# Layer 1 of a four-layer graph network: gathers by rows of 128 edges instead of by items, into a ring of 128 rows

## What is computed

```python
def _L1_gnn_ref(x, edge_index, W_msg, b_msg, W_upd, b_upd):
    messages = jax.nn.relu(x @ W_msg.T + b_msg)
    src, dst = (edge_index[0], edge_index[1])
    aggregated = jax.ops.segment_sum(messages[src], dst, num_segments=x.shape[0])
    updated = jax.nn.relu(aggregated @ W_upd.T + b_upd)
    return updated + x
# layer 2, on the result x: msg_in = concat(h[src], h[dst], edge_attr_64), two matmuls with a gate
...
h = jnp.maximum(_layernorm(x, axis=-1), 0.0)
x = x + _L1_gnn_ref(h, edge_index, L1_gnn_W_msg, L1_gnn_b_msg, L1_gnn_W_upd, L1_gnn_b_upd)
```

## Time and profile before

| | |
|---|---|
| median of 3 runs | 6709.26 us (6705.14 to 6719.22) |
| profiled execution, time | 6689.83 us |
| profiled execution, span | 6688.1 us |
| layer 1, edges: first gather issued to the node update's start | 1957.49 to 3217.80 us |
| layer 1, gathers: 832, first to last issue | 1957.5 to 3201.1 us |
| granted TensorE clock, mean of the execution | 0.755 |

### The profile page before, as it was taken

How to read it: one execution, slowest core, us unless ns; L and a number is a source line. 1 busy time by engine, 2 the same in 40 slices (tenths; PEclk the granted TensorE clock), 3 DMA queues, 4 the chain that set the end, 5 groups by cost and what they waited for, 6 DMA issues and landing times. The chain is left out here.

```text
span 6688.1 us, 110212 instructions
## 1 busy us (share of the span) xinstructions
PE 4492.3 (67%) x20750; PEld 3303.1 (49%) x20751; DVE 3446.8 (52%) x10783; ACT 1916.5 (29%) x5540; POOL 3778.8 (56%) x3395
## 2 busy tenths in 40 slices
PE   0588788888545555555767776767766667666767
PEld 0466566666334444444555565556554444344444
DVE  2555655556452323233656565555564555555554
ACT  1222222222112222222322222222233333333333
POOL 1488888888636666666255554555524455445542
PEclk9755555555567776677888989898887888888888
DMA  9355555555624544454344444444422222222221
GB/s 301 50 71 71 71 71 71 71 71 71 95 82 149 158 152 152 152 154 154 101 130 138 136 138 134 138 135 138 134 62 53 38 38 39 37 38 39 38 37 41
DMA packets 820582, 660.16 MB, mean 99 GB/s; under 512 B 441865, under 2 KB 707955, under 8 KB 819962
## 3 DMA queue, kind: packets, MB, share of 16 engines
q0 software_dynamic: 217184, 287.62, 21.6%
q1 hardware_dynamic: 602682, 340.12, 18.5%
q10 hardware_dynamic: 640, 31.60, 1.4%
HBM read 464.78 MB, written 225.68 MB: 103 GB/s over the span
## 5 line engine op out<-in xcount | busy, mean ns | idle before, releaser
L651 POOL DMA_INDIRECT G<-table,src_it x2496 | 2412.6, 967 | 2129.2 <-issue 657.3
L1369 DVE TENSOR_TENSOR big<-bank,big 128x129 f32 (+2 forms) x2496 | 882.5, 354 | 1548.0 <-remote 636.0
L623 POOL DMA_INDIRECT sums<-work,idx x832 | 1284.1, 1543 | 318.0 <-issue 179.2
L781 PE MATMUL bank<-work 128*128 128x128 f32 x1664 | 622.4, 476 | 197.7 <-DVE work L1416 111.0
L877 PE MATMUL bank<-big,oh 128*128 128x320 f32 x1664 | 683.5, 559 | 27.2 <-DVE big L1369 18.0
L1021 ACT ACTIVATE work<-bank,work 128x128 f32<-128x128 f32 x832 | 305.4, 367 | 1066.5 <-PE bank L773 725.1
L781 PEld LDWEIGHTS bank<-work 128*128 128x128 f32 x1664 | 407.4, 304 | 387.8 <-DVE work L1416 241.8
L1356 DVE TENSOR_TENSOR oh<-iota,rel_it 128x512 f32<-128x512 f32 x625 | 429.1, 687 | 295.6 <-remote 135.9
L773 PE MATMUL bank<-big,work 128*128 x1664 | 580.8, 451 | 0.0
L728 PE MATMUL bank<-We,work 64*128 64x256 f32 x1664 | 337.6, 539 | 348.0 <-ACT work L1000 233.8
L877 PEld LDWEIGHTS bank<-big,oh 128*128 128x128 f32 x1664 | 373.6, 242 | 247.8 <-issue 129.4
(11 more groups left out here) (230 smaller groups left out, 7751.5 us busy)
## 6 DMA issues: line engine op xcount, KB each, us to landing
e_pre<-work SPq DMA_DIRECT2D x208, 512.0 KB
work<-e_pre SPq DMA_DIRECT2D x208, 512.0 KB
G<-e_src SPq DMA_DIRECT2D x832, 64.0 KB
G<-table,src_it POOLq DMA_INDIRECT x2496
work<-e_a SPq DMA_DIRECT2D x832, 32.0 KB
e_a<-in_edge_attr_dram ACTq DMA_DIRECT2D x1, 25000.0 KB, 103.2
sums<-work,idx POOLq DMA_INDIRECT x832
work<-e_a SPq DMA_DIRECT2D x832, 4.0 KB
```

The source lines that it names most:

```text
L623: pool.indirect_dma_start(sums[k % COPIES], bass.IndirectOffsetOnAxis(ap=idx[:, k:k + 1], axis=0), z_out[:, k, :], None, compute_op=ALU.ad ...
L651: pool.indirect_dma_start(G[:, k, 0:wid], None, tab, bass.IndirectOffsetOnAxis(ap=src_it[:, n:n + 1], axis=0)).then_inc(quad_in[k // 4], 16)
L781: t.matmul(bank[4 + s % 2][:, 0:P], same[:, s % 4, :], scaled[:, s % 4, :], start=True, stop=True).then_inc(ph["sum_done"], 1)
L1369: v.tensor_tensor(to, ps, to, ALU.add).then_inc(EDGE[layer]["acc_done"], 1)
```

## The change

Layer 1 gathers each of the 782 rows once, into a ring of 128 rows `G1`, of 129 columns each, which lies in `big` behind the accumulator (columns 6528 to 23039). The column of ones for the degrees is set in `G1` at the layer's start instead of in `G` at the kernel's start. PE reads an item's row at slot row % 128, with row numbers that it loads from `row_row` into registers: 16 for four quads at a time (`top`), and one more in each step (the last item's row), against which it waits on a new semaphore, `rows_landed`. POOL counts that semaphore up: behind the four gathers of group g it waits for the landing of group g-2 and adds 4 (`relay`). From group 32 on it waits before a group until g-19 quads are summed. The source nodes of a row stand in a new table `src_row` in the right half of `G`; the set-up gets two more DMAs on POOL's queue (and a clear of 128x128), seven more transposes on PE, seven more copies and one more cast on DVE. Layers 2 and 3 keep their gathers; only the counts that they wait for change.

```diff
+R1 = 128
+ROWS4 = (ROWS + 3) // 4
...
+        src_row = G[:, 0:CHUNKS, P:2 * P].bitcast(I32)
+        G1 = big[:, 6528:6528 + R1 * 129].rearrange("p (r f) -> p r f", f=129)
...
             for c in range(CHUNKS):
                 at = bass.IndirectOffsetOnAxis(ap=it_ai[:, c:c + 1], axis=0)
...
+            whole = ROWS // P
+            pool.wait_ge(tail_ready, 2)
+            pool.dma_start(m_r[:, 0:whole * P].rearrange("p (c e) -> p c e", e=P),
+                           rows128(e_src)[0:whole * P, :].rearrange("(c p) e -> p c e", p=P)).then_inc(meta_rows, 16)
+            pool.dma_start(m_r[0:ROWS - whole * P, whole * P:META], rows128(e_src)[whole * P:ROWS, :]).then_inc(meta_rows, 16)
...
+            def gather_rows(tab):
+
+                def relay(g):
+                    n = min(4, ROWS - 4 * g)
+                    pool.wait_ge(quad_in[g % 4], 64 * (g // 4) + 16 * n)
+                    pool.sem_inc(rows_landed, n)
+
+                for g in range(ROWS4):
+                    if g >= R1 // 4:
+                        pool.wait_ge(EDGE[1]["agg_done"], g - (R1 - NB - 3) // 4)
+                    for r in range(4 * g, min(4 * g + 4, ROWS)):
+                        pool.indirect_dma_start(G1[:, r % R1, 0:D], None, tab,
+                                                bass.IndirectOffsetOnAxis(ap=src_row[:, r // P, r % P:r % P + 1], axis=0)).then_inc(quad_in[g % 4], 16)
+                    if g >= 2:
+                        relay(g - 2)
+                relay(ROWS4 - 2)
+                relay(ROWS4 - 1)
...
+                regs = [pe.alloc_register(f"grow_{k}") for k in range(RING)]
+
+                def top(item):
+                    pe.load(regs, row_row[0:1, bass.ds(item + (LEAD - 4), RING)])
...
-                        pe.wait_ge(quad_in[(k - 1) % 4], QUAD_BEFORE[1] + landed(64, 4, q, k, 1))
+                        last = pe.value_load(row_row[0:1, bass.ds(4 * q + (LEAD - 1), 1)], min_val=0, max_val=ROWS - 1)
+                        pe.wait_ge(rows_landed, last + 1)
...
                         for j in range(4):
-                            n = (k - 1) % 4 * 4 + j
-                            mm = t.matmul(bank[2 * o + j // 2][:, j % 2 * wid:(j % 2 + 1) * wid], oh[:, n, :], G[:, n, 0:wid], start=True, stop=True)
+                            slot = pe.snap(regs[k % 4 * 4 + j], min_val=0, max_val=ROWS - 1) % R1
+                            mm = t.matmul(bank[2 * o + j // 2][:, j % 2 * wid:(j % 2 + 1) * wid], oh[:, (k - 1) % 4 * 4 + j, :],
+                                          at(G1, slot), start=True, stop=True)
```

More of the change, by code:

```diff
@@ L195, in gnn_layers @@
         attr_in = [sem(f"attr_in{k}") for k in range(RING)]
-        quad_in, QUAD_BEFORE = [sem(f"quad_in{k}") for k in range(4)], [None] + [64 * (QUADS // 4) * q for q in range(3)]
+        quad_in, QUAD_BEFORE = [sem(f"quad_in{k}") for k in range(4)], [None, None] + [
+            [64 * (QUADS // 4) * q + 16 * sum(min(4, ROWS - 4 * g) for g in range(k, ROWS4, 4)) for k in range(4)] for q in range(2)]
         e_out, e_back = [sem(f"e_out{k}") for k in range(2)], [sem(f"e_back{k}") for k in range(2)]
@@ L603, in _ @@
             m_w = big[:, 2 * META:3 * META]
+            m_r = big[:, 7 * META:8 * META].bitcast(I32)
+            g.memset(m_r[:, META - P:META], 0).then_inc(tail_ready, 1)
             for c in range(CHUNKS):
@@ L643, in _ @@
                 g.memset(big[:, 0:NBT * wid], 0.0)
+                if layer == 1:
+                    g.memset(G1[:, :, 128:129], 1.0)
                 barrier(pool)
                 tab, wid = table[layer], table[layer].shape[1]
-                freed = EDGE[layer][(None, "agg_done", "eg_done", "prod_done")[layer]]
+                if layer == 1:
+                    gather_rows(tab)
+                    barrier(pool)
+                    barrier(pool)
+                    continue
+                freed = EDGE[layer][(None, None, "eg_done", "prod_done")[layer]]
                 for n in range(ITEMS):
@@ L659, in _ @@
             t = nc.tensor
-            pe.wait_ge(const_ready, 3)
+            pe.wait_ge(const_ready, 4)
             pe.wait_ge(counts_ready, 1)
@@ L668, in _ @@
             mm.then_inc(meta_T, 1)
-            m_f = big[:, 3 * META:6 * META]
+            m_f = big[:, 3 * META:7 * META]
             pe.wait_ge(meta_rel, 1)
-            for q in range(3 * CHUNKS):
+            for q in range(4 * CHUNKS):
                 b = q % 6
@@ L1252, in _ @@
             m_w = big[:, 2 * META:3 * META]
-            m_f = big[:, 3 * META:6 * META]
-            dve.wait_ge(meta_rows, 16 * 3 * CHUNKS)
+            m_r = big[:, 7 * META:8 * META].bitcast(I32)
+            m_f = big[:, 3 * META:7 * META]
+            dve.wait_ge(meta_rows, 16 * (3 * CHUNKS + 2))
             link(v.tensor_scalar(it_off[:], it_b[:], float(P), None, ALU.mult))
@@ L1261, in _ @@
             dve.drain().then_inc(meta_rel, 1)
-            for q in range(3 * CHUNKS):
+            for q in range(4 * CHUNKS):
                 dve.wait_ge(meta_T, q + 2)
-                to = (src_it, rel_it, w_it)[q // CHUNKS]
+                to = (src_it, rel_it, w_it, src_row)[q // CHUNKS]
                 c = q % CHUNKS
-                v.tensor_copy(to[:, c * P:(c + 1) * P], bank[1 + q % 6][:, 0:P]).then_inc(meta_out, 1)
-            dve.wait_ge(meta_T, 3 * CHUNKS + 2)
+                to = to[:, c, :] if q >= 3 * CHUNKS else to[:, c * P:(c + 1) * P]
+                v.tensor_copy(to, bank[1 + q % 6][:, 0:P]).then_inc(meta_out, 1)
+            dve.wait_ge(meta_T, 4 * CHUNKS + 2)
             for half, (lo, hi) in enumerate(((0, 4), (4, CHUNKS))):
```

23 lines of the change are left out of this document (12 added, 11 removed).

## The result

The changed kernel takes **6792.51 us** (median of 4, 6778.81 to 6799.11) where the kernel before takes 6707.20 (median of 4): 1.0125 of it, with an interval of 1.0100 to 1.0151. It is 85 us slower; 6770 was predicted, with 6560 to 6850 as the range. The compared profiled executions have spans of 6777.1 and 6688.1 us, 89.0 apart. Layer 1's edges go from 1967.61 to 3301.28, 1333.7 us instead of 1260.3: +73.4. They begin 10.1 us later, and everything behind them takes 5.5 us longer.

The account below looks back on a forecast made before the run. Layer 1 was taken as bound by handshakes, PE's reports arriving late while POOL issues gathers. 165 + 5 + 999 + 144 + 4 = 1317, less 1260.3 = +57, with set-up +61: 6770 us, range 6560 to 6850.

Parts of the forecast that it names:

- the pause lets it through: Layer 1: PE's reports arrive late while POOL issues back to back; POOL's 1.0 us stop per 5.99 us quad releases them.
- Term 1: Layer 1's start, filling the ring of 128: 12 quads summed in 165 us, 5 us more until the 33rd group.
- My bound for PE standing still: Layer 1's start: PE stops after two quads until POOL pauses; 10 quads to catch up, 23 us of release, +122.
- Term 2: Layer 1's middle: each group waits for one more quad, 164 groups at 6.09 us, 999 us.
- Term 3: Layer 1 after POOL's last group: 32 quads without gathers at 4.5 us, 144 us, and 4 to the barrier.
- Term 4: PE's register loads and work: 0 while covered in the middle, 0.4 us a quad at the end, up to 1.2.
- Term 5: Set-up before layer 1: seven transposes 1.5 us, two DMAs and a clear 2.5 us, together 4 us.
- Term 6: Layer 1's 50 fewer gathers: 62 us of POOL's time and 3.3 MB less traffic, worth nothing further.
- The signs: Checks: 128 gathers in 165 us beside 12 sums (2 to 20), groups 6.1 us apart, last gather 148 us before barrier.
- Fair sharing: Layer 1: POOL's run costs PE nothing, PE goes at 4.9 us a quad; -229 us, 6480; chance 0.20.
- The relay is the pause: Layer 1: POOL waits some 1 us a group for landings, letting PE's reports through; -53 us, 6656; chance 0.10.
- The register loads are on the path: Layer 1: loads between transposes and sums delay the sums; 0.5 us for 164 quads, 82 us slower, 6852; chance 0.10.

Follow-up runs that it names:

- experiment 6: Changed kernel with 128 unbroken gathers, then POOL waiting for g-3 quads, and PE's products doubled in the first eight quads: 6786.37 us, the kernel before 6690.45.
- experiment 3: Changed kernel gathering a quarter of its rows: 5329.47 us; items in the ring of 128, no register loads, a quarter gathered: 5284.10; the kernel before 5511.00.
- the kernel with a quarter of the rows: Changed kernel gathering only the first row of each group of four, 196 gathers instead of 782: 5329.47 us, the kernel before 5511.00.
- experiment 4: Changed kernel with POOL's waits and memset pauses varied over five stretches of groups, on chip 10: 6806.95 us, the kernel before 6683.83.
- the short lag: Changed kernel with POOL waiting for g-3 quads from the fifth group on: 5459.16, 5456.56, 5457.72 us; 0.9901, 0.9893, 0.9899 of the kernel before.
- the five-stretch kernel: Changed kernel with POOL's waits and memset pauses varied over five stretches of groups: 5510.45 us on chip 5 (before 5511.00), 6806.95 on chip 10 (before 6683.83).

## Why the prediction held, point by point

**The reading of the profile** was right in its coincidences. PE's reports come late while POOL issues without a break, PE never waits for data, and the layer goes in lock step. The test is that the same program has none of it on the prompt chips, where the result has the other sign. The forecast leant on a profile from a late chip, and the pair was timed on one; on a prompt chip its direction would have been wrong. What was wrong is the words "the pause lets it through". In numbers it is a balance, in which a length of time counts and not the event. Two readings give the same size for it, 1.40 us (the first two points together, and the third); the fourth gives what is left beside it:

- Release comes 20.3 us after the end of a run of 128 gathers (2127.36 to 2147.67), 3.5 after one of 20 and 1.9 after one of 8. From 20 to 128 it grows by 16.8/108 = 0.156 us a gather.
- POOL's gathers come 1.248 us apart. With 0.156 that is 1.40 us.
- Each PE instruction in a run costs 1.40 us (experiment 6).
- Groups of four pass in lock step at 5.99, 6.09, 6.07 and 6.03 us: 4 x 1.40 = 5.60, which leaves 0.4 to 0.5 for all 36 instructions of a quad.

So on a late chip it looks as if something that POOL and PE share takes 1.40 us for each gather. POOL fills it every 1.25 us, and while it is behind, one PE instruction passes per gather. That is an inference. It gives a number that was not used for it: with one memset a group, 5.87 - 5.60 = 0.27 us are left of the 0.47 that a quad needs (6.07 - 5.60), 0.57 of a quad for each of 32 groups, 18 quads; 17 passed. (For the kernel before, 832 x 1.40 + 208 x 0.47 = 1263 us, beside 1260.3; but that is only 208 groups of 6.07 us, the pace of lock step again, and no test.)

**Term 1, the fill: too small.** I predicted 12 quads in 165 us and 5 us more until the 33rd group. There were 3, and the group came at 213.8 us (1967.61 to 2181.43): +44. The step that failed is the choice of 14 us a quad. It was read from the first two quads of a run, of which the first had passed before anything was behind, and the second was let out by the end of the run. Neither was a pace. The pace in a run is 50.4 us a quad. My bound for PE standing still, with 23 us until release, was the nearer one: release took 20.3. By it the 33rd group would have come 233 us after the first, with 2 quads in the run. (With its own terms that bound adds up to +124 and not +122.)

**Term 2, lock step:** 164 groups x 6.09 = 999 us predicted, 994.5 measured. Right; that the pace agrees to the hundredth is luck, since its 0.1 us stood for the relay and was taken from no row.

**Term 3, the last quads:** 32, as predicted. They took 125.4 us (3175.86 to 3301.28) and not 148: 3.9 us each with the barrier and not 4.5 without it. This gave back half of what term 1 had too little.

**Term 4, PE's additions:** nothing in lock step was predicted; 6.09 is what was forecast for rows against 5.99 before, and the 0.1 us had been put to the relay. Which of the two it is, if not the difference between two executions, is not shown. Bare they cost 0.22 us (experiment 3), less than the 0.4 that I took, and far from the upper bound of 1.2. The load of one register, for which I had put in the 0.554 us of a single one on DVE, took 0.304 us on PE in the changed kernel and 0.622 in the kernel with a quarter of the rows (medians of 208).

**Term 5, set-up:** 4 us predicted. DVE's wait for the transfers ends at 207.40 instead of 202.47, of which 2.8 us were there at 128 us already and 2.2 come with the two new DMAs. PE's transposes take 5.91 instead of 4.4 us, and DVE's part with them is 2.0 us longer:

```profile
203.31 0.92 POOL L619 DMA_DIRECT2D big<-e_src  x1
204.19 0.60 POOL L621 DMA_DIRECT2D big<-e_src  x1
...
210.75 5.91 PE L714 MATMUL bank<-ident,big 128*128 128x128 f32 x28 [47.31 <-DVEq L1307]
```

Together 4.2 us. The other 5.9 of the 10.1 lie in the first 128 us (2.8) and between 217 and 302 us (3.1). They are not explained, and neither are the 5.5 us behind the layer. Between executions the start of the layer moves too: 1965.11 in the kernel of experiment 4, 1968.10 in that of experiment 6, with the same set-up.

**Term 6 and the sum:** +57 for the layer and +61 in all were predicted; the profiles show +73.4 and +89.0, the medians +85. In the layer +44, -4.5 and -23 make up some 16 us between forecast and profile: two errors, of which the second hides half of the first, so the total is nearer than its terms. The gathers that are saved were worth nothing here, as said: PE was 32 quads behind when the last was issued.

**The signs** that were named: POOL's 128 gathers took 160 us, 3 quads of sums passed beside them (2 to 20 had been named), groups followed 6.09 us apart, and the last gather came 125 us before the barrier and not 148. One sign failed: ACT's waits for `t_done` did not end with the run. Of its 44 waits for an unknown sender 40, with 392.8 of the 558.8 us, lie in the lock step behind it, where PE's update still comes up to 9 us late.

**The rivals.** *Fair sharing* is false here and true on chips 4, 5 and 11. There a run of 128 gathers disturbs nobody, and the layer takes 1008.8 us (1031 worked out). Its -229 did not come out even so: it was reckoned against the 1260.3 us of a late chip, and on chip 4 the change gains 62. The rule that queues with work take turns in a DMA engine (the Trainium skill, page "DMA: Bandwidth & Descriptors", section "Queues, rings and completion order") gave that result; it speaks of data, and the data are on time on both kinds of chip. *The relay is the pause*: no, 0.6 us of waits in 196. *The register loads are on the path*: they would have made the pace 6.6 us, and it is 6.09; a kernel without them was not run on a late chip.

What I had no case for is that the answer depends on the chip. The profile of before held a hint: the program has nothing that makes the end of a matmul be reported 16 us later.

## What to carry to other kernels

A pace must be read from the middle of a long stretch in the same condition, not from its first two events: an average over the start of a run took 14 us for what is 50.4. When an engine off the critical path is let loose, ask what had been paid for by its stops: a ring eight times as deep took POOL's stops away for 128 gathers, and PE all but stood still for 160 us. And where a profile shows completed work reported late, time the change on more than one chip: this one is 1.2% slower on one kind and 1.1% faster on another, and the short lag, which takes 0.990 on prompt chips, should be about even on a late one. Its layer on a late chip can only be put together from experiment 6: 195.25 groups x 6.07 and 67 us are 1253 us, beside 1260.3 before and 1333.7 for the changed kernel, and the start that is 10 us later takes the 7 us back. The short lag from the fifth group on was never timed on a late chip. By the balance above a wait that follows the items and not the rows would bring the layer to 782 x 1.40 + 208 x 0.47 = 1193 us, an estimate; it was not tried.

## What the runs showed of the hardware

**Chips differ by a fifth on one program.** The kernel before takes 5511 to 5517 us on three chips and 6684 to 6707 on the others, with nearly the same time until layer 1 (layer 1 of the changed kernel starts at 1965.91 on chip 4, 1967.61 on the first) and the same time of a gather (944 ns median). Of the 1324 us between these two spans of the changed kernel 325 lie in layer 1's edges and 998 behind them (2478 us on chip 4 and 3476 on the first).

**On a late chip a MATMUL with its weight load costs 2.80 us, 1.40 for each instruction, beside unbroken gathers**, whatever its width (experiment 6). SP is slowed to much the same pace: its four loads with the six register instructions between them take 12.6 us instead of 2.2, some 1.3 us for each of the ten (a register instruction of SP is recorded with 0.70 us there, median, and with 0.053 on chip 4). The register instructions of DVE (0.057 us) and of PE (0.097 us, medians) take the same on both kinds of chip. The gathered data are not late: in the changed kernel the last of the 128 gathers has moved its bytes before 2130 us, 18 us before PE's report comes.

**On a late chip records are missing.** The trace of the changed kernel holds 49 475 updates of semaphores by DMAs on the first chip and 110 139 on chip 4; the five-stretch kernel 51 010 on chip 10 and 110 031 on chip 5. All four traces from late chips lack about half of these records, and none of the ten from prompt chips does. So late updates and lost records go together. The Trainium skill, page "NOTIFIC — the notification-queue block", section "Overflow: three behaviours, one of which stalls the engine", states that the block which writes such records holds its producers back when its inner buffers fill, and that this can throttle an engine. The traces agree with it in that the cost goes by instruction and not by work. The lost records don't fit it as it stands: by that section the inner buffers hold back rather than lose a record, and records are lost where the ring behind them is full. That it is the cause is not shown: the profiled execution is no slower than the others (6778.81 us, and 6789.74 to 6799.11), and whether those wrote such records is not on record. What makes a chip a late one stays open.
